# A fused model kernel: where the first attention's ring entries stand, and how its inverse row sums reach the outputs' layout

## The reference

```python
x = x + attn_a(layernorm(x), Wq, Wk, Wv, Wo, bo)       # 16 heads of 64, causal
x = x + moe(layernorm(x), Wr, W1, b1, W2, b2)          # 8 experts, top 2, capacity
x = x + gated_attention(layernorm(x), ...)
x = x + moe(layernorm(x), ...)
x = x + mamba(layernorm(x), ...)
x = x + glu(layernorm(x), ...)
x = x + attn_b(layernorm(x), ...)
x = x + glu(layernorm(x), ...)

def attn_a(x, Wq, Wk, Wv, Wo, bo):
    q, k, v = heads(x @ Wq), heads(x @ Wk), heads(x @ Wv)
    scores = causal(einsum('bhid,bhjd->bhij', q * 64 ** -0.5, k))
    out = einsum('bhij,bhjd->bhid', softmax(scores), v)
    return join(out) @ Wo + bo
```

## Time and profile before

| | us |
|---|---|
| runs, median (lowest to highest) | 3054.18 (3046.66 to 3077.77) |
| the profiled execution | 3079.38 |
| its span | 3077.3 |
| PE busy | 2633.8 |
| DVE busy | 2024.4 |
| ACT busy | 1688.5 |
| POOL busy | 901.4 |
| PE busy on L300 between 0 and 1200 us (248 products) | 37.8 |

### The profile page before, as it was taken

How to read it: one execution, slowest core, us unless ns; L and a number is a source line. 1 busy time by engine, 2 the same in 40 slices (tenths; PEclk the granted TensorE clock), 3 DMA queues, 4 the chain that set the end, 5 groups by cost and what they waited for, 6 DMA issues and landing times.

```text
span 3077.3 us, 54379 instructions
## 1 busy us (share of the span) xinstructions
PE 2633.8 (86%) x20224; PEld 1718.3 (56%) x20224; DVE 2024.4 (66%) x4632; ACT 1688.5 (55%) x3282; POOL 901.4 (29%) x931
## 2 busy tenths in 40 slices
PE   7999889988998999679888558787975879999988
PEld 4666656665666666664446545666765532333325
DVE  5666556655655554247885146999999768888845
ACT  4676456645664566232221227868775336677762
POOL 1000020002000200344132564767777212322321
PEclk9999999999999999889999787898989989999999
DMA  5000000000000000211001211121211450101000
GB/s 181 2 2 2 1 10 1 2 1 10 2 2 1 10 2 21 59 52 28 5 13 34 63 52 42 59 71 66 77 62 69 161 173 2 57 8 51 2 2 28
DMA packets 79941, 114.22 MB, mean 37 GB/s; under 512 B 10109, under 2 KB 48172, under 8 KB 79680
## 3 DMA queue, kind: packets, MB, share of 16 engines
q1 hardware_dynamic: 71488, 97.07, 9.6%
q0 software_dynamic: 8192, 13.67, 1.6%
HBM read 77.66 MB, written 35.78 MB: 37 GB/s over the span
## 4 chain that ended last, share of the span: by engine, by line
PE 27%; issue 12%; POOL 8%; DVE 6%; another core or an unknown queue 4%; ACT 3%; DMA 0%; SPq 0%; POOLq 0%; ACTq 0%; DVEq 0%
POOL arena L2083 7%; PE ps L2312 4%; PE ps L1385 3%; PE ps L1191 3%; PE ps L2283 2%; PE ps L2270 2%; PE ps L688 2%; PE ps L2274 2%; ACT arena L2392 2%; PE ps L677 2%; PE ps L1394 1%; DVE Wqkv L2433 1%; PE ps L1182 1%; PE ps L2321 1%
## 5 line engine op out<-in xcount | busy, mean ns | idle before, releaser
L387 ACT ACTIVATE arena<-ps 128x512 f32<-128x512 f32 (+1 forms) x640 | 334.2, 548 | 404.7 <-PE ps L291 387.4
L499 DVE CUSTOM_DVE_ANT_0 arena<-ps,causal 128x512 f32<-128x512 f32 (+3 forms) x512 | 282.1, 588 | 327.8 <-PE ps L278 284.4
L400 ACT ACTIVATE arena<-arena 128x640 f32<-128x640 f32 (+7 forms) x512 | 394.2, 770 | 38.7 <-DVE arena L499 34.7
L2433 DVE TENSOR_REDUCE Wqkv<-ps 128x2 f32<-128x1024 f32 (+2 forms) x320 | 345.2, 1113 | 88.0 <-PE ps L2274 60.7
L291 PE MATMUL ps<-ident,arena 128*128 128x128 f32 x2304 | 347.8, 284 | 46.1 <-ACT arena L400 32.7
L2083 POOL TENSOR_TENSOR arena<-arena,W 128x1024 f32<-128x1024 f32 x128 | 332.6, 2617 | 137.0 <-DVE W L2035 137.0
L1791 PE MATMUL ps<-rope,arena 128*128 128x128 f32 x2048 | 283.5, 301 | 97.5 <-ACT rope L1930 50.4
L2392 ACT ACTIVATE arena<-ps 128x1024 f32<-128x1024 f32 (+1 forms) x320 | 291.8, 939 | 134.1 <-PE ps L2283 131.1
L291 PEld LDWEIGHTS ps<-ident,arena 128*128 128x128 f32 x2304 | 255.8, 143 | 162.2 <-issue 86.1
L312 PE MATMUL ps<-arena,rope 128*64 128x128 f32 x4608 | 341.2, 284 | 0.0
L1791 PEld LDWEIGHTS ps<-rope,arena 128*128 128x128 f32 x2048 | 268.6, 213 | 128.0 <-issue 71.1
(11 more groups left out here) (265 smaller groups left out, 4275.8 us busy)
## 6 DMA issues: line engine op xcount, KB each, us to landing
select<-c_rows SPq DMA_DIRECT2D x64, 512.0 KB, 3.6
arena<-q_dram SPq DMA_DIRECT2D x4, 2048.0 KB, 8.9
arena<-k_dram SPq DMA_DIRECT2D x4, 2048.0 KB, 14.0
q_dram<-arena SPq DMA_DIRECT2D x24, 256.0 KB, 3.7
k_dram<-arena SPq DMA_DIRECT2D x24, 256.0 KB, 3.8
arena<-slots_in SPq DMA_DIRECT2D x8, 640.0 KB, 6.8
slots_out<-arena SPq DMA_DIRECT2D x8, 640.0 KB, 4.3
slots_in<-select SPq DMA_DIRECT2D x4, 640.0 KB, 6.3
```

What stands on the lines that cost most here:

```text
L387: nc.scalar.activation(k.probT[:, n % 2, b0 * P:(b0 + nb) * P], k.ps[:, 4 + m % 2, 0:nb * P], ACT.Copy)\
L400: nc.scalar.activation(k.prob[:, i % 2, h, 0:w], k.prob[:, i % 2, h, 0:w], ACT.Exp, bias=k.neg_max[:, i % 2, h:h + 1], scale=-1.0, accum_o ...
L499: ins = nc.vector.tensor_tensor_reduce(k.prob[:, i % 2, h, 512 * g:512 * g + w], k.ps[:, banks[h], 0:w], k.causal[:, first:first + w], 1.0 ...
L2433: nc.vector.tensor_reduce(k.least[:, g, As[0]:As[-1] + 1, i % 4, c, :], k.ps[:, 2 * slot:2 * slot + 2, 0:len(As) * w].rearrange("p h (a w) ...
```

## The change

The five rarer ring entries move to the ends of steps, behind transposes and values, and to other steps: `out` from 3 and 5 to 2 and 5, `tokens` from step 3 to 2, `rt`, `logits` and `pos` to step 2 of the sequence's pairs 1, 2 and 3. The pieces of routing on DVE are spread anew, the scatters move one pair later, and PE's slot after `pos` is free once DVE has read it (`pos_read`) and not at the end of the piece (`scatter_idx`); the later mixing stage uses that semaphore too.

The reciprocals no longer pass POOL, PE and ACT's copy. DVE writes them as head by block; ACT issues a DMA that stores them into a DRAM tensor of 2 x 4 x 128 (at the end of the step two behind blocks 3 and 7), and one step later two DMAs that load each head's 512 numbers into 64 partitions, with a second buffer for the second group. DVE normalises five steps behind the block, not three.

```diff
-A_T_FIRST = (4, 6, 7, 9, 11, 15, 18, 22)
-A_INV = (14, 27)
-A_PIECES = 22
-A_ABSENT = 5
+A_T_FIRST = (0, 1, 2, 4, 6, 9, 12, 16)
+A_PIECES = 20
+A_NORMAL_LAG = 5
...
-A_TOKENS_PAIR, A_TOKENS_STEP = 6, 3
+A_TOKENS_PAIR, A_TOKENS_STEP = 6, 2
-A_OUT_STEPS = (3, 5)
-A_ROUTE_ENTRIES = {(1, 5): "rt", (1, 6): "logits", (2, 4): "pos"}
-A_ROUTE_PIECES = {(0, 6): (0, 1), (0, 7): (2,), (1, 3): (3,), (1, 4): (4,), (1, 6): (5,), (1, 7): (6,), (2, 3): (7, 8),
-                  (2, 4): (9,)}
+A_OUT_STEPS = (2, 5)
+A_ROUTE_ENTRIES = {(1, 2): "rt", (2, 2): "logits", (3, 2): "pos"}
+A_ROUTE_PIECES = {(0, 5): (0, 1), (0, 6): (2,), (0, 7): (3,), (1, 0): (4,), (2, 3): (5,), (2, 5): (6,), (2, 6): (7,),
+                  (2, 7): (8,), (3, 3): (9,)}
...
@@ pe_attention_a
-            pe.wait_ge(k.M["scatter_idx"], p + 1)
+            pe.wait_ge(k.M["pos_read"], p + 1)
...
-        def spread_inverse(q, group):
-            m = A_INV[group]
-            pe.wait_ge(sm["rr"], q * 2 + group + 1)
-            wait_piece_bank(q, m)
-            for b in range(4):
-                mm = nc.tensor.transpose(k.ps[:, 4 + m % 2, b * P:(b + 1) * P], k.inv_wide[:, b, :], k.ident[:])
-            mm.then_inc(sm["t_ps"], 1)
...
+            q, n = a_prev(p, prev, i, 1)
+            r, u = a_prev(p, prev, i, 2)
...
             if ("tokens", p // 8 + 1) in A_AT and p % 8 == A_TOKENS_PAIR and i == A_TOKENS_STEP:
                 tokens(p // 8 + 1)
...
             if entry == "pos":
                 pe_route_positions(nc, k, pe, k.M, p // 8 - 1)
-            q, n = a_prev(p, prev, i, 1)
-            r, u = a_prev(p, prev, i, 2)
...
-            if r is not None and u % 4 == 3:
-                spread_inverse(r, u // 4)
...
@@ act_attention_a
-        def take_inverse(q, group):
-            m = A_INV[group]
-            act.wait_ge(sm["t_ps"], a_piece_count(q, m, q == p and group == 1))
-            if not (q == 0 and group == 0):
-                act.wait_ge(sm["o_norm"], q * 2 + group)
-            nc.scalar.activation(k.inv_spread[:], k.ps[:, 4 + m % 2, :], ACT.Copy).then_inc(sm["t_out"], 1)
+        def store_inverse(q, group):
+            act.wait_ge(sm["inverse"], q * 2 + group + 1)
+            if q > 0:
+                act.wait_ge(sm["inv_in"], 32 * (q * 2 + group - 1))
+            act.dma_start(k.inv_dram[group].rearrange("h i q -> q (h i)"), k.inv_sum[:, group, :],
+                          allow_slow_non_contiguous=True).then_inc(sm["inv_out"], 16)
+
+        def load_inverse(q, group):
+            act.wait_ge(sm["inv_out"], 16 * (q * 2 + group + 1))
+            if q > 0:
+                act.wait_ge(sm["o_norm"], q * 2 + group - 1)
+            for h in range(2):
+                act.dma_start(k.inv_spread[64 * h:64 * h + 64, group, :],
+                              k.inv_dram[group][h].rearrange("i q -> (i q)").partition_broadcast(64)).then_inc(sm["inv_in"], 16)
...
+            q, n = a_prev(p, prev, i, 2)
+            if q is not None and n in (3, 7):
+                store_inverse(q, n // 4)
+            q, n = a_prev(p, prev, i, 3)
+            if q is not None and n in (3, 7):
+                load_inverse(q, n // 4)
...
@@ dve_attention_a
-            dve.wait_ge(sm["t_out"], a_piece_count(q, A_INV[group], q == p and group == 1))
+            dve.wait_ge(sm["inv_in"], 32 * (q * 2 + group + 1))
             nc.vector.tensor_tensor(k.attT[:, q % 8, group * 512:(group + 1) * 512],
-                                    k.ps[:, 6 + group, :], k.inv_spread[:], ALU.mult).then_inc(sm["o_norm"], 1)
+                                    k.ps[:, 6 + group, :], k.inv_spread[:, group, :], ALU.mult).then_inc(sm["o_norm"], 1)
...
-            r, u = a_prev(p, prev, i, 3)
+            r, u = a_prev(p, prev, i, A_NORMAL_LAG)
...
@@ pool_attention_a
-    def spread(p, group):
-        pool.wait_ge(sm["inverse"], p * 2 + group + 1)
-        pool.wait_ge(sm["t_ps"], p * A_PIECES + (6, 15)[group])
-        pool.sem_inc(sm["gate"], 1)
-        nc.gpsimd.tensor_copy(k.inv_wide.rearrange("p a (h d) -> p (a h) d", h=2),
-                              k.inv_sum[:].unsqueeze(2).to_broadcast([P, 8, 64])).then_inc(sm["rr"], 1)
...
-        if p >= 8 and p % 8 == 2:
+        if p >= 8 and p % 8 == 3:
             pool_scatter(nc, k, pool, k.M, p // 8 - 1, range(0, 6))
-        if p >= 8 and p % 8 == 3:
-            pool_scatter(nc, k, pool, k.M, p // 8 - 1, range(11, 16))
+        if p >= 8 and p % 8 == 4:
+            pool_scatter(nc, k, pool, k.M, p // 8 - 1, range(6, 16))
...
@@ dve_route_place
     ch.settle()
+    dve.sem_inc(sm["pos_read"], 1)
...
-        k.inv_wide = arena.take([4, P])
-        k.inv_spread = arena.take([512])
+        k.inv_spread = arena.take([2, 512])
+        k.inv_dram = [nc.dram_tensor(f"inverse{g}", [2, 4, P], F32, kind="Internal").ap() for g in range(2)]
```

More of the change, by code:

```diff
@@ L281, in wait_piece_bank @@
         def wait_piece_bank(q, w):
-            if q == 0 and w - 2 in (2, 3, 5):
+            if q == 0 and w < 2:
                 return
@@ L331, in pair @@
                     project_values(p + 1, a_banks("project", p, i))
+            q, n = a_prev(p, prev, i, 1)
+            r, u = a_prev(p, prev, i, 2)
+            pieces = a_pieces(n) if q is not None and n < 8 else []
+            parts = (len(pieces) + 1) // 2 if pieces else 1
+            part = 0
+            for at, (m, b0, nb) in enumerate(pieces):
+                transposes(q, n, m, b0, nb)
+                if r is not None and at % 2 == 1 and part < parts - 1:
+                    values(r, u, parity if r == p else 1 - parity, part, parts)
+                    part += 1
+            if i == 9:
+                project_out(p // 8, 0)
+            while r is not None and part < parts:
+                values(r, u, parity if r == p else 1 - parity, part, parts)
+                part += 1
             if ("tokens", p // 8 + 1) in A_AT and p % 8 == A_TOKENS_PAIR and i == A_TOKENS_STEP:
@@ L1138, in wait_entry @@
         else:
[L1139 removed]
+            pe.wait_ge(moe["pos_read"], b + 4)
     def base(b):
```

67 lines of the change are left out of this document (19 added, 48 removed).

## The result

The changed kernel takes 3392.05 us (median of 4 runs, 3377.10 to 3395.20) where the kernel before takes 3065.67 us (4 runs, 3046.66 to 3077.77): a ratio of 1.106, interval 1.098 to 1.114. The forecast was 3008 us with a range to 3075; the time lies far above both. Its profiled execution took 3395.20 us, the span is 3393.2, so 315.9 us more than the span of before.

A forecast was written before the change was run, and what follows sets the result against it. PE was taken as the bound, 93% busy in the first attention. Terms -34 + 3 + 6 - 22 = -47 us give 3032.4 on the profiled execution, 3007.6 on the median; own range 2985 to 3020, stated range to 3075.

The forecast's parts named there:

- the landing of the store: First attention, inverse's store to DRAM: lands in 4.2 us (2.5 to 7.2), so ACT waits for nothing before the loads.
- Rival 1: Store lands late, ACT's queue head blocks PE and DVE: 3074 us at 6.0 us landing, 3150 at 7.2; chance 0.22.
- the formula: Late store's cost: landing L beyond covers of 4.5 and 5.4 us in a pair's two halves, summed, times 32.
- The transposes, -34: First attention: four PE transposes fewer in each of 64 groups, 0.53 us a group, 34 us saved on saturated PE.
- +3: Step 5 of a pair: PE's next transposes still wait for the second exponential, charged 0.1 us a pair, 3 us.
- +6: Step 6 of a pair: issuing two loads on ACT delays its copy, 0.2 us a pair, 6 us (0 to 11).
- Rival 2: PE's cut is not the path's, copies and exponentials set the pace: transposes give a third, 3027 us; chance 0.15.
- The ring entries, -22: First attention: moved entries remove PE waits of 29.1 us, three quarters counted, 22 us saved (bounds 0 and 32).
- The new waits it charged for the second output projection: Scores of step 6 need the bank of the output projection in step 5: some 0.4 us, three times.
- Rival 3: The ring's waits on PE only move, before scores or through DVE's routing pieces delaying maxima: 3029 us; chance 0.15.
- The landing of the loads: DVE's normalisation five steps behind: second group's loads issued by 177.2, wanted about 181.1, so just in time.
- What it named as proof of being wrong: PE's transposes wait for ACT 1 us or more a pair, a DMA as releaser; or named waits return before scores.

The follow-up runs named there:

- e7_sp_queue: Changed kernel with the inverse's store and loads issued from SP's queue instead of ACT's; 2955.71 us, ratio 0.9991 to the kernel before.
- f1_sp_own_64B: Changed kernel with DMAs on SP's queue, the store's 4-byte runs 64 bytes apart, loads reading fixed numbers; 3029.65 us (before 3046.86).
- e5_own_64B: Changed kernel with the store's 1024 4-byte runs written 64 bytes apart, loads reading fixed numbers; 2902.35 us, 0.979 of the kernel before.
- e3_contiguous: Changed kernel with the store as 128 runs of 32 bytes, transposition left out; 2905.02 us, ratio 0.9816 to the kernel before.
- e1_ring_only: Kernel before with only the moves of ring entries, routing pieces and scatters, inverse as before; 2928.22 us, ratio 0.9898 to the kernel before.
- g3: Changed kernel with 32-byte store runs, transposition left out, run again in a later group; 3025.67 us, ratio 0.9935 to the kernel before.
- g1: Kernel before with only the moves of ring entries, routing pieces and scatters, run again in a later group; 3024.28 us, ratio 0.9923.
- e2_dma_only: Changed kernel with ring entries, pieces and scatters where they stood before, inverse by DMA; 3257.50 us, ratio 1.1011 to the kernel before.

## Why the prediction was wrong, point by point

**The step that failed is the landing of the store.** The prediction put it as: 3.6 us, the usual landing, plus 64 packets an engine at 10 ns, 4.2 us, with bounds of 2.5 and 7.2. It is 10.7 (e7_sp_queue), 11.0 as ACT sees it. The term for the packets was right in size: 0.6 us was expected, and the engines are busy about 0.5 us each. The bounds came from the packets' price, and the time lies in something that has no row in the trace of before: between the last packet and the signal, when small writes fall close together. The sums lie so that 16 numbers of one row, from 16 neighbouring partitions, share 64 bytes. The upper bound assumed that packets set the end, and so it bound nothing. The nearest row, 64 KB into DRAM in 3.6 us, was a store of 16 rows of 4 KB; nothing in it is like this.

The Trainium skill says of this place, for DMAs that GpSimd issues, that the semaphore isn't updated until the target memory has confirmed the last byte, and that this receipt makes up most of a DMA's fixed 2 us ("DMA: Bandwidth & Descriptors", "Anatomy of one DMA — SWDGE (gpsimd) path"). The trace agrees in kind, with 10 us and not 2 between packets and signal. By that page's fixed cost and price of a packet the prediction's estimate was 2.7 us: f1_sp_own_64B measured 2.8, where no two writes share 64 bytes. Its rule against a strided last dimension pointed the right way; the 65536 packets bear it out, but e5_own_64B shows that their number by itself is not what costs. What it says of reads and rewrites below 512 bytes doesn't give the size either, since writes of 4 bytes, 64 bytes apart, land in 2.8 us here.

**Rival 1 came true**, with its mechanism, its place and its formula, at a size outside its bounds. With L = 11.0 the formula gives ((11.0 - 4.5) + (11.0 - 5.4)) x 32 = 387 us; less the gain of 47 that is +340, where 326 was measured between the medians. The sum is close in part by luck, since two errors offset each other. The formula charged too much idle time: the waits behind the stores come to 327.6 us in all, with the issue of the loads in them, and PE's new idle time is 231 us. The cover was larger than 4.5 and 5.4 us: ACT issued the store at 307.93, before the exponentials of its step were through, and had work until 314.56, 6.6 us. And the clock adds what the formula doesn't have. The 256 transposes were 39 us of busy time, yet busy time is 81 us more, so some 120 us were added; 105 of them lie in the attention's own products (the transposes L287 took 379.7 us for 347.8, the values 375.1 for 341.2), which fits PE at a lower clock behind its own waits. The rest lies in later stages and isn't explained. A chance of 0.22 and a worst price of 3150 us were too kind to a store whose price no row showed.

**The transposes, -34, with +3 and +6.** With a store that lands in time the inverse's part gains 23.2 us in the first group (e3_contiguous against e1_ring_only) where these three make -25, and nothing in another (g3 against g1), where the stalls of DVE and ACT beside the scatters are longer. The trace of before has such stalls too (36.4 us on DVE), and no step of the prediction asked what releases them. The -25 was met with wrong parts. The +6 for issuing the loads on ACT should have been 0: in e3_contiguous they lie beside a copy and an exponential (286.98 to 288.08). And a group of transposes is worth less than the 0.53 us from its start to the next start: step 1 of a pair takes 4.90 us in e1_ring_only (scores from 269.02 to 273.92) and 4.46 in e3_contiguous (298.19 to 302.65), step 5 takes 4.75 and 4.31, so 0.44 each time, 28 us for 64. Most pairs without a ring entry took 34.02 to 34.23 us and take 33.13 to 33.44, so on average a little less than 28 us comes. Rival 2, by which a third of the 34 would come, falls: the wait for the exponential kept its size (29.5 us in both), and two thirds came.

**The ring entries, -22.** 28.9 us came in one group and 24.4 in another (3048.72 less 3024.28); the earlier trace rows holds 29.1, of which the prediction took three quarters. The new waits it charged for the second output projection don't show. Rival 3, by which the waits would only move, falls.

**The landing of the loads, just in time.** In e7_sp_queue, where the store lands after 10.7 us and the loads go out at once, DVE waits for them twice, 10.1 us in all up to 1215 us. So the place is less tight than the prediction had it.

**What it named as proof of being wrong** is what the trace shows: PE's transposes wait for ACT by far more than 1 us a pair, with the store as the one that holds ACT up.

## What to carry to other kernels

Before a transposition is given to a DMA, look how close together its small pieces fall in the target: 64 bytes apart, 1024 writes of 4 bytes land in 2.8 us, and side by side, 16 to 64 bytes, they take 10.7, nearly all of it after the engines are done. A price that no row shows has no upper bound made from other rows; where a waiting instruction heads a busy engine's queue, put the DMA and its wait on a queue with nothing behind it: with that the ratio in one group was 1.00 (e7_sp_queue), where it was 1.10 with ACT waiting (e2_dma_only, which has the moved entries less, worth 0.01). And count an idle engine's clock too: by the sum above about a third of this loss was not waiting but PE's products taking longer.

## What the runs showed that was not expected

- A store's signal can come 10 us after its packets: the engines' share was 0.47 for one us and then 0.03 in the 10 us up to the signal.
- Writes of 4 bytes cost nothing by being small: 1024 of them, 64 bytes apart, landed in 2.8 us in the median, less than the 3.6 us of a 64 KB store. A store of 8 rows of 512 bytes landed in 1.2 us.
- The landing is not in proportion to the density: 2.8, 3.0, 3.3, 6.3 and 10.7 us for 1, 2, 4, 8 and 16 writes to 64 bytes (4 with half as many writes).
- A DMA's issue on ACT's queue ran beside ACT's copies and exponentials: 0.37 us for a store, 0.45 and 0.62 for two loads, that cost nothing.
- After 5.8 us without work PE's granted clock was 0.50 for at least 4 us, and 1.00 again by 330 us.
- One kernel's time differed by 3.6% from group to group (2957.11 and 3064.91 us for the kernel before), and a change's gain too: 1.8% in one and 0.65% in another for one kernel (e3_contiguous), with stalls of DVE and ACT of up to 17.6 us beside POOL's scatters in the second and none in the first.
